# One core, Mamba block with a routed expert layer: norms applied by ScalarE, additions as identity products, a second running sum, gating on VectorE, one copy of the routed rows

## What is computed

```python
h = x + mamba(layernorm(x, g1, b1))            # expand to 512 channels, 16 states per channel
m = gelu(layernorm(h, g2, b2) @ mlp_w1.T + mlp_b1) @ mlp_w2.T + mlp_b2
x = layernorm(x + (h + m))                     # no gain, no bias
# expert layer: softmax over 8 experts, the two best of each token
routed = sum over the two: weight * down_e(silu(gate_e(x)) * up_e(x))
shared = silu(x @ sg.T) * (x @ su.T) @ sd.T
out = layernorm(x + routed + shared)

# mamba: xz = x @ in_proj.T; causal convolution of 4 taps on half of it, silu -> xc
# dt, B, C from xc; the recurrence for each channel d and state n:
#   h = exp(dt * A[d, n]) * h + dt * xc * B[n];   y += C[n] * h
# y = (y + xc * D_param) * silu(z);  y @ out_proj.T
```

## Time and profile before

| | us |
|---|---|
| median of 3 executions | 6505.38 (6500.32 to 6505.66) |
| the profiled execution | 6514.27 |
| its span, first to last instruction | 6512.5 |
| mean granted TensorE clock | 0.770 |
| VectorE busy | 4832.9 (74%) |
| GpSimd busy | 4603.2 (71%) |
| TensorE busy (matmul) | 4338.0 (67%) |
| ScalarE busy | 2740.6 (42%) |

### The profile page before, as it was taken

How to read it: one execution, slowest core, us unless ns; L and a number is a source line. 1 busy time by engine, 2 the same in 40 slices (tenths; PEclk the granted TensorE clock), 3 DMA queues, 4 the chain that set the end, 5 groups by cost and what they waited for, 6 DMA issues and landing times. The chain is left out here.

```text
span 6512.5 us, 72002 instructions
## 1 busy us (share of the span) xinstructions
PE 4338.0 (67%) x18880; PEld 3104.8 (48%) x18880; DVE 4832.9 (74%) x7430; ACT 2740.6 (42%) x4258; POOL 4603.2 (71%) x2862
## 2 busy tenths in 40 slices
PE   4566666667767766667776666777666677676653
PEld 2344444455545544445554544555445455454543
DVE  5877888888877778777777777878877778777521
ACT  3444444444444433444444444444344443444211
POOL 4577766666666677876667787766777867787644
PEclk7576777778778878778877777887878888887876
DMA  6755211122222222332222233221234322343345
GB/s 183 219 183 187 91 36 36 35 62 80 80 80 67 67 67 67 96 97 75 64 69 50 82 105 92 72 68 56 57 107 115 83 87 72 114 127 91 98 111 137
DMA packets 361969, 596.83 MB, mean 92 GB/s; under 512 B 36560, under 2 KB 184272, under 8 KB 361440
## 3 DMA queue, kind: packets, MB, share of 16 engines
q1 hardware_dynamic: 312416, 524.97, 26.4%
q0 software_dynamic: 49152, 67.27, 5.1%
HBM read 372.60 MB, written 219.50 MB: 91 GB/s over the span
## 5 line engine op out<-in xcount | busy, mean ns | idle before, releaser
L473 POOL TENSOR_TENSOR dBx<-dtx,Bbc 128x1024 f32<-128x1024 f32 x1024 | 2434.3, 2409 | 806.4 <-DVE hs L978 767.4
L978 DVE TENSOR_TENSOR_SCAN hs<-ps,dBx 128x512 f32<-128x512 f32 x2048 | 2420.0, 1208 | 255.0 <-issue 135.8
L759 PE MATMUL ps<-ident,hs 128*128 128x128 f32 x8192 | 1601.1, 346 | 874.6 <-DVE acc L992 485.2
L626 ACT ACTIVATE ps<-dt,A 128x512 f32<-128x512 f32 x2048 | 1400.3, 689 | 1323.8 <-DVE hs L978 1307.2
L759 PEld LDWEIGHTS ps<-ident,hs 128*128 128x128 f32 x8192 | 1250.3, 180 | 1282.7 <-DVE acc L992 680.9
L992 DVE SCALAR_TENSOR_TENSOR acc<-ps,C_tok,acc 128x512 f32<-128x512 f32 x1920 | 1368.4, 734 | 554.1 <-PE ps L759 530.1
L907 PE MATMUL ps<-post_tmp,wx 128*128 128x128 f32 x2560 | 453.4, 343 | 118.1 <-issue 118.0
L543 POOL DMA_INDIRECT fx<-Y_slots,slots x256 | 406.7, 1589 | 170.3 <-DMA fx<-shared 86.3
L907 PEld LDWEIGHTS ps<-post_tmp,wx 128*128 128x128 f32 x2560 | 427.0, 254 | 151.1 <-issue 145.8
L526 POOL DMA_INDIRECT X_slots<-xs,slots x256 | 255.1, 996 | 260.0 <-DVE slots L1117 178.9
L888 PE MATMUL ps<-ident,xin 128*128 128x128 f32 x640 | 152.3, 383 | 340.3 <-DMA xin<-X_slots 339.8
(11 more groups left out here) (148 smaller groups left out, 5773.0 us busy)
## 6 DMA issues: line engine op xcount, KB each, us to landing
Bbc<-B_scratch SPq DMA_DIRECT2D x512, 256.0 KB
wx<-in_experts SPq DMA_DIRECT2D x320, 384.0 KB
X_slots<-xin SPq DMA_DIRECT2D x26, 2056.0 KB, 19.7
Y_slots<-xin SPq DMA_DIRECT2D x26, 2048.0 KB
xin<-X_slots SPq DMA_DIRECT2D x320, 128.5 KB
Y_slots<-mT SPq DMA_DIRECT2D x320, 128.0 KB
xt<-in_x SPq DMA_DIRECT2D x32, 512.0 KB, 4.0
shared<-xt SPq DMA_DIRECT2D x32, 512.0 KB
```

What stands on the lines that cost most here:

```text
L473: pool.tensor_tensor(dBx[u % 3][:], dtx[b % 2][:, 2 * h:2 * h + 2, :], Bbc[g % NBB][:, n % CH:n % CH + 1, :].broadcast_to([P, 2, T]), ALU. ...
L626: act.activation(psA[s % 2][:], dt[b % 2][:, j, :], ACT.Exp, scale=A[:, j, n:n + 1]).then_inc(s_dA, 1)
L759: i = pe.transpose(psH[w % 2][:, j * P:(j + 1) * P], hs[(n * CT + j) % NHB][:, t * P:(t + 1) * P], ident[:])
L978: dve.tensor_tensor_scan(hs[s % NHB][:], psA[s % 2][:], dBx[s // 2 % 3][:, s % 2, :], 0.0, ALU.mult, ALU.add).then_inc(s_scan, 1)
```

## The change

- The norms are applied by ScalarE (`activation` Identity with scale = rs and bias = -mean*rs, four for each norm). GpSimd keeps the statistics' small steps and gets one more pair for each norm (the negated mean, its product with rs). The second norm is written once.
- Additions move to TensorE: `c*D` is a product with a diagonal matrix `D_diag` (made once) in the PSUM bank of y; `x`, `h1`, `b2` and the normed row of the shared expert come in as products with the identity or with a row of ones ahead of the accumulating products. VectorE's three residual sums go. ScalarE copies the first (`h1`) and the last (`shared`) out of PSUM; the second isn't written at all, and VectorE's statistics and ScalarE's norm read it in PSUM.
- States 0 to 7 and 8 to 15 go to two running sums, both opened by ScalarE (`OPENED = (0, 8)`), in three buffers; both are turned into the same PSUM bank and so added. VectorE weighs 14 states in place of 15.
- The gate product moves from GpSimd to VectorE and reads y in PSUM.
- There is one copy of the routed rows. The four scatters of the second choice wait until the first four have landed and until GpSimd has put the second weight into column 256.
- The clearing DMAs, the store of `shared` and the store of the output are issued by ScalarE's queue in place of SyncE's.
- All places of `AT` are new.

The diff, cut to its core (of the tables only some rows):

```diff
-    "DVE_scan": [-1.02, -0.66, 0.44, 0.54, 0.61, 0.61, 0.61, 1.13, 1.33, 1.57, 4.26, 6.08, 8.14, 8.17, 9.47, 9.55,
...
-        56.28],
-    "SP_clear": [-37.09, -36.96, -35.8, -35.8, -35.8, -15.26, -9.9, 16.04, 16.04, 28.1, 38.4, 42.27, 44.02],
+    "ACT_clear": [-149.74, -149.74, -120.5, -63.13, -61.58, -58.78, -56.39, -44.7, -42.62, -42.37, -29.56, -28.54,
+        -18.41],
+    "ACT_pre": [-43.32, -35.45, -31.95, -30.73, -26.98, -25.74, -24.71, -23.66, -22.94, -22.51, -21.59, -18.98,
+        -17.83, -15.8, -12.47, -11.93, -11.8, -6.18, -6.18, -2.27, -1.06, -1.06],
+    "DVE_scan": [-2.42, -2.42, 4.13, 4.13, 4.19, 4.35, 5.02, 5.02, 5.02, 5.22, 5.51, 8.41, 10.2, 10.2, 12.09, 12.09,
...
+        45.14, 45.7, 46.72, 47.13, 49.01, 49.01, 49.98, 50.63, 51.65, 52.14, 55.9, 58.19, 60.69, 61.76, 63.68, 63.68,
+        63.68],
+    "POOL_pre": [-57.58, -7.07, 1.08],
+    "POOL_post": [103.49, 108.76, 117.68, 125.35, 125.35, 125.45, 128.45, 129.69, 130.77, 131.01, 131.01],
...
+    OPENED, NACC = (0, NS // 2), 3
...
             def pre():
...
+                    pool.tensor_scalar(nb["pre"][:], mv["pre"][:, :, 0], -1.0, None, ALU.mult).then_inc(s_var_pre, 1)
...
+                    pool.tensor_tensor(nb["pre"][:], nb["pre"][:], rs["pre"][:], ALU.mult).then_inc(s_rstd_pre, 1)
-                    for t in range(NTB):
...
-                        pool.tensor_scalar(tok_pre[b % 2][:, t, :], xt[b % NX_IN][:, t, :], mv["pre"][:, t, 0:1],
-                                           rs["pre"][:, t:t + 1], ALU.subtract, ALU.mult).then_inc(s_norm_pre, 1)
...
                     for c in range(2):
+                        if c:
+                            yield b
+                            pool.wait_ge(s_scattered, (b * 2 + 1) * NTB * 16)
+                            pool.tensor_scalar(xs[:, :, D], top2[:], 1.0, None, ALU.mult).then_inc(s_second, 1)
...
+            def clear():
+                for i, rows in enumerate((X_slots[0], X_slots[1], Y_slots[0], Y_slots[1])):
+                    width = 2 * rows.shape[1]
+                    for k in range(CLEARS):
+                        yield i
...
+                        act.dma_start(rows.rearrange("(p n a) d -> p n (a d)", p=P, a=2)[:, k * n:(k + 1) * n, :],
...
+                        act.activation(tok_pre[b % 2][:, t, :], x[:, t, :], ACT.Identity, scale=rs["pre"][:, t:t + 1],
+                                       bias=nb["pre"][:, t:t + 1]).then_inc(s_norm_pre, 1)
...
+                        act.activation(h1[:, 2 * q:2 * q + 2, :], psG[q][:].rearrange("p (t d) -> p t d", d=D),
+                                       ACT.Copy).then_inc(s_h1, 1)
...
+                        act.activation(x[:, 2 * q:2 * q + 2, :], psY[:].rearrange("p (t d) -> p t d", d=D),
+                                       ACT.Copy).then_inc(s_sum, 1)
...
+                    act.dma_start(shared[b], x[:].rearrange("p t d -> p (t d)")).then_inc(s_kept, 16)
...
+                        pe.matmul(psY[:], D_diag[:, j, :], c[:, j, :], start=True, stop=False, skip_group_check=True)
                         for t in range(NTB):
-                            i = pe.transpose(psY[:, t * P:(t + 1) * P], acc[b % 2][:, t, j * P:(j + 1) * P], ident[:])
+                            for n in OPENED:
+                                i = pe.matmul(psY[:, t * P:(t + 1) * P], sums(b, n)[:, t, j * P:(j + 1) * P], ident[:],
+                                              is_transpose=True, start=False, stop=(t, n) == (NTB - 1, OPENED[-1]),
+                                              skip_group_check=True)
...
+                                if k == 0:
+                                    pe.matmul(psG[q][:, t * D:(t + 1) * D], ident[:], x[:, 2 * q + t, :], start=True,
+                                              stop=False)
...
+                                if k == 0:
+                                    o = psG[q][:, t * D:(t + 1) * D]
+                                    pe.matmul(o, one_row[:], b2[:], start=True, stop=False)
+                                    pe.matmul(o, ident[:], x[:, 2 * q + t, :], start=False, stop=False)
+                                    pe.matmul(o, ident[:], h1[:, 2 * q + t, :], start=False, stop=False)
...
+                            pe.matmul(psY[:, t * D:(t + 1) * D], ident[:], h1[:, 2 * q + t, :], start=True, stop=False)
...
-                        dve.scalar_tensor_tensor(out=c[:, j, :], in0=c[:, j, :], scalar=D_half[:, j:j + 1],
-                                                 in1=psY[:], op0=ALU.mult, op1=ALU.add).then_inc(s_y_plus, 1)
-                    for q in range(2):
-                        yield b
-                        dve.wait_ge(s_out_mm, per_batch(b, q, 2))
...
-                        dve.tensor_tensor(h1[:, 2 * q:2 * q + 2, :], psG[q][:].rearrange("p (t d) -> p t d", d=D),
-                                          x[:, 2 * q:2 * q + 2, :], ALU.add).then_inc(s_h1, 1)
...
+                        dve.wait_ge(s_silu_z, per_batch(b, j, CT))
+                        dve.tensor_tensor(c[:, j, :], psY[:], post_tmp[:, j, :], ALU.mult).then_inc(s_gated, 1)
```

More of the change, by code:

```diff
@@ L197, in build @@
         dbc = sb("dbc", [NX, T])[:]
-        xs = [sb(f"xs{i}", [P, NTB, ROW]) for i in range(2)]
-        h1 = xs[0][:, :, 0:D]
+        xs = sb("xs", [P, NTB, ROW])
+        h1 = xs[:, :, 0:D]
         mT = sb("mT", [P, KD, T])
@@ L646, in post @@
                         act.activation(post_tmp[:, j, :], psG[j % 2][:], ACT.Tanh, scale=0.5).then_inc(s_tanh_z, 1)
+                    for q in range(2):
+                        yield b
+                        act.wait_ge(s_out_mm, per_batch(b, q, 2))
+                        if q == 0 and b:
+                            act.wait_ge(s_scattered, b * 2 * NTB * 16)
+                            act.wait_ge(s_down_s, b * 2)
+                        act.activation(h1[:, 2 * q:2 * q + 2, :], psG[q][:].rearrange("p (t d) -> p t d", d=D),
+                                       ACT.Copy).then_inc(s_h1, 1)
+                    for t in range(NTB):
+                        yield b
+                        if t == 0:
+                            act.wait_ge(s_rstd_post, (b * 2 + 1) * 2)
+                            act.wait_ge(s_gated, (b + 1) * CT)
+                        act.activation(tok_post[:, t, :], psG[t // 2][:, t % 2 * D:(t % 2 + 1) * D], ACT.Identity,
+                                       scale=rs["post"][:, t:t + 1], bias=nb["post"][:, t:t + 1]).then_inc(s_norm_post, 1)
                     for k in range(KD):
@@ L659, in post @@
                             s_gelu, 1)
+                    for t in range(NTB):
+                        yield b
+                        if t == 0:
+                            act.wait_ge(s_rstd_post, (b + 1) * 4)
+                            act.wait_ge(s_m2_mm, (b + 1) * 2)
+                        act.activation(xs[:, t, 0:D], psG[t // 2][:, t % 2 * D:(t % 2 + 1) * D], ACT.Identity,
+                                       scale=rs["post"][:, t:t + 1], bias=nb["post"][:, t:t + 1]).then_inc(s_norm_post, 1)
                     for k in range(KD):
@@ L693, in results, with finish @@
                                            scale=xin[p % 2][:, i, D:ROW]).then_inc(s_yo, 1)
+            def finish():
+                for b in range(PERIODS):
+                    for f in fins_in[b]:
+                        for t in range(NTB):
+                            yield b
+                            if t == 0:
+                                act.wait_ge(s_rstd_fin, (f + 1) * 2)
+                            act.activation(fx[:, t, :], fx[:, t, :], ACT.Identity, scale=rs["fin"][:, t:t + 1],
+                                           bias=nb["fin"][:, t:t + 1]).then_inc(s_norm_fin, 1)
+                        act.wait_ge(s_norm_fin, (f + 1) * NTB)
+                        act.dma_start(out[f].rearrange("(t p) d -> p t d", p=P), fx[:]).then_inc(s_stored, 16)
             weave((scan(), AT["ACT_scan"]), (weigh(), AT["ACT_weigh"]), (pre(), AT["ACT_pre"]),
-                  (post(), AT["ACT_post"]), (experts(), AT["ACT_experts"]), (results(), AT["ACT_results"]))
+                  (post(), AT["ACT_post"]), (experts(), AT["ACT_experts"]), (results(), AT["ACT_results"]),
+                  (finish(), AT["ACT_finish"]), (clear(), AT["ACT_clear"]))
+            act.wait_ge(s_stored, 16 * NB)
         @block.tensor
@@ L937, in _ @@
             dve.wait_ge(s_consts, CONSTS)
+            dve.wait_ge(s_halved, 5)
+            for j in range(CT):
+                dve.tensor_scalar(D_diag[:, j, :], ident[:], D_half[:, j:j + 1], None, ALU.mult).then_inc(s_diag, 1)
             dve.wait_ge(s_A_exp, 1)
@@ L982, in weigh @@
                 for b in range(NB):
-                    for n in range(1, NS):
+                    for n in range(NS):
+                        if n in OPENED:
+                            continue
                         for t in range(NTB):
                             w = (b * NS + n) * NTB + t
```

(2 more changed lines are left out.)

340 lines of the change are left out of this document (149 added, 191 removed), and 30 rows, old and new, of the table AT.

## The result

The changed kernel takes 6632.2 us (median of 4 runs, 6627.5 to 6637.3) against 6505.1 us for the kernel before, 1.0197 times as long, 95% interval 1.0179 to 1.0215. The forecast was 6105 with a range to 6350. So the sign was wrong, and the size by 527 us.

The account below looks back on a forecast made before the run. No engine was full; VectorE's work plus the waits of its in-order stream were taken to set the time. Terms -231 - 248 - 72 + 30 + 30 + 0 + 110 - 20 = -401 gave 6105 us, range 5890 to 6350.

Parts of the forecast that it names:

- TensorE's work: Added products, 15 us a batch at most, cancel against shorter waits for GpSimd's norms: 0, bounds -200 and +300.
- The waits that the additions were set against: TensorE's idle for GpSimd's norms, 228.9 and 167.1 us in all, 12 us per batch, was to shrink.
- The relief as a whole: The terms for VectorE, gap, finishing batches, scatters, ScalarE and tail taken together: -511 us.
- scatters: On GpSimd, the second four scatters wait for the first four to land: +30 us, bounds 0 and 166.
- VectorE's work: Less weighing, no residual sums, cheaper c*D, all counted as time: -231 us, bounds 0 to -231.
- The gap between batches: The 24.6 us without a scan between two batches shrinks by the new order: -248 us, bounds 0 and -372.
- GpSimd and the finishing batches: GpSimd's lighter work saves 6 us in each of 12 finishing periods: -72 us, bounds 0 and -126.
- late exps: In ScalarE's in-order stream, norms waiting for statistics hold the scans: +30 us, bounds 0 and +96.
- The start: Clears on ScalarE's queue delay the first scan (+65) and the next three batches (+45): +110 us, bounds 0 and +364.
- The tail: After the last scan, shorter norms and a shorter post stage: -20 us, bounds 0 and -40.
- Rival (C): TensorE becomes the bound, turns of scans queueing behind post products: +399 us, 6905, chance 0.08.
- The sign that I named for being wrong: Gap still over 20 us, TensorE past 85% of a period with growing turn waits, or late ScalarE exps.

Follow-up runs that it names:

- e1: The changed kernel without all of TensorE's added products (their sums missing from the output): 6255.0 us, ratio 0.9609.
- e7: The kernel before, with twelve idle identity products a batch put ahead of its second MLP products, output unchanged: 6677.9 us, ratio 1.0268.
- e3: The changed kernel with the 52 clearing DMAs issued by SyncE again, at their old places: 6577.2 us, ratio 1.0104.
- h1: The changed kernel with clears on SyncE and the second residual sum back on VectorE and GpSimd, output complete: 6379.5 us, ratio 0.98.

## Why the prediction was wrong, step by step

**TensorE's work: the step that failed.** It read "I let the two cancel: 0", with bounds -200 and +300. The two were added products, 15 us a batch as an upper value, against waits for GpSimd's norms. Measured, the additions alone are +377 us (e1): nine tenths of the added work in the path, where the upper bound had two thirds. What the shorter waits gave back no run separates. Two errors are in it. First, I judged the cost by TensorE's share of a whole period (132.3 of 187.9) and did not cut the period at the stage that gets the products, where e1 and e7 show almost every added microsecond in the path. Second, the count: "20 products of 256 columns (0.379)" took one instruction for each, while the groups show two (x256 for four products a batch in 32 batches). Groups of the changed kernel:

```profile
L869 PE MATMUL ps<-b,one_row 1*128 1x256 f32 x256 | 88.8, 426 | 11.3 <-ACT post_tmp L658 11.3
...
L871 PE MATMUL ps<-xs,ident 128*128 128x256 f32 x256 | 76.2, 379 | 0.0
...
L820 PE MATMUL ps<-xc,D_diag 128*128 128x512 f32 x256 | 131.0, 593 | 0.7 <-ACT mT L708 0.7
```

L829 in the earlier trace rows said the same (x1024 for 16 products in 32 batches). The 15 us a batch still came out near, 418 / 32 = 13.1 in e1, because the union of overlapping records is well below the sum of their durations. That is luck: two records a product were left out, and the overlap was too. In the chain a product took 0.53 us and not 0.379.

**The waits that the additions were set against** did go: no wait of TensorE for GpSimd's norms is left, and it waits 67.2 and 34.7 us for ScalarE's, in place of 228.9 and 167.1. What that was worth is part of e1's time and not measured by itself.

**The relief as a whole: sign right, size 60%.** VectorE, gap, finishing, scatters, ScalarE and tail were to give -511 us. e1 less e3's 55 us for the clears would be 6200, so -305 was got, if the two effects add up (no run has both edits). So the miss of 527 us has two main parts, TensorE's 377 and 206 of missing relief, less 55 that the clears cost under their forecast. This sum closes by the way it is made and proves nothing further.

**VectorE's work: right in its groups, less in time.** Weighing lost 80 us of 94 and the three sums went. But the busy time, a union in which neighbours overlap, fell by only 151 us, and h1 shows that putting one sum back costs some 8 us. "I take all of it" was too much.

**The gap between batches: right as a gap, not as time.** At the boundary after the batch above, VectorE runs these scans:

```profile
3288.43 1.21 DVE L1024 TENSOR_TENSOR_SCAN hs<-ps,dBx 128x512 f32<-128x512 f32 x1
...
3302.59 1.22 DVE L1024 TENSOR_TENSOR_SCAN hs<-ps,dBx 128x512 f32<-128x512 f32 x1
...
3317.46 3.45 DVE L1024 TENSOR_TENSOR_SCAN hs<-ps,dBx 128x512 f32<-128x512 f32 x3 [1.19 <-ACT ps L609]
...
3325.59 4.54 DVE L1024 TENSOR_TENSOR_SCAN hs<-ps,dBx 128x512 f32<-128x512 f32 x4
```

The first of the three scans at 3317.46 is the last of its batch (the starts of every 64th scan show it) and the other two open the next, so nothing stands between the batches, and 4.7 us without a scan follow where there were 24.6. But the longest break now lies inside the batch: 12.9 us from the end of the 57th scan (3288.43) to the 58th (3302.59), with the routing and its wait of 5.99 us for the ranks in it. The order was also not quite what the prediction read from the table: the second of the next batch's dt steps (3316.66 on GpSimd) runs behind four scatters and not ahead of seven.

The -248 did not follow. In e1, where no addition interferes, the period of batch 8 is

```profile
1496.50:1677.60 181.10, 133.91 (x590) 96.08 (x590) 141.94 (x212) 95.55 (x153) 97.57 (x58) 0.79 0.22 72
```

so VectorE is idle 39.2 us in it, against 36.5 in batch 8 before and 187.9 - 147.9 = 40.0 in batch 9. As means by kind of period (without experts, with them, with finishing) VectorE is idle 32.3, 38.2 and 47.4 us before and 30.2, 38.6 and 38.3 in e1. The idle time of the gap did not go; it stands elsewhere in the period, and only the finishing periods lost some. This is read from the profiles; a kernel with the old gap and all else new would need a table of its own and was not tried.

**GpSimd and the finishing batches: right in size.** GpSimd is busy 3583.6 (forecast 3500 to 3600). A finishing period was 14.6 us above a plain one and is 7.7, that is 6.9 less where 6 were forecast.

**ScalarE: right in work, its wait misplaced.** It is busy 3140.8 us (near 3160). A norm took 0.56 to 0.59 us where 0.5 was taken. What the forecast feared, late exps, is 126.2 us in all (92.1 before). What it did not price are the copies that VectorE's statistics wait for, 203.8 us.

**The start: mechanism right, size half.** +55 us in time (e3), +110 forecast. The first part (+65) came as 51 (57 by e3). The +45 for the next batches did not come: a clear that stood alone held the queue 0.38 us, and only in a burst did it cost more (the four from 107.68 held it 0.38, 0.60, 3.45 and 6.34 us). The Trainium skill (DMA: Bandwidth & Descriptors, section Issuing engines are not separate DMA queues) calls the sequencer's time to initiate a DMA usually small beside the transfer. For the clears that stood alone the trace agrees; for the burst it does not, where eight issues held ScalarE 37.53 us.

**The tail: right**, -38 within its bounds, at twice the -20 taken.

**Rival (C)** had the place and the sign, and 0.08. It made TensorE the bound through turns queued behind post products, and decided at 85% of a period. Neither holds: the batch-8 period stands at 149.4 of 194.8, 77%, and the waits for turns fell. What decides is a chain, not a load. Its price (+399) missed too: it took 480 for the added work where 377 came, 110 for the start where 55 came, and nothing for the gap and the finishing periods. The sign that I named for being wrong would not have shown it.

Beside this stands a rule of the Trainium skill (Perfetto Trace Analysis, sections Identifying the Most-Contended Engine and Optimization Strategy): the engine with the highest occupancy is to be optimized first, within each regime where a kernel has several, and for TensorE the shares of its weight loads and of peak arithmetic are to be taken, not that of its matmuls. Before the change VectorE's busy share was the highest beside the weight loads', over the span (74% against 48%) and in the stretch of batch 4 (81% against 54%). Taking 151 us of work from it still came with a loss, because the share does not say who waits for the work where it goes. The waits of VectorE above say it.

## What to carry to other kernels

Before moving work to the engine with spare time, cut the period at the stage that will hold it and ask who waits for the result: twelve products cost 6.4 us a batch ahead of the MLP's and 0.5 ahead of the turns of the scans. The MLP's residual sum, made by VectorE on the way out of PSUM with GpSimd preparing the other operand, cost some 8 us in all; as identity products in front of the main product it cost 206. Where an in-order engine waits for a small result, look at what stands ahead of that result on the other engine: one reordering gave 108 us with no work removed. And a break that is closed in one place has to be looked for in the others before its time is counted as gained.

## What the runs showed of the hardware that was not expected

A VectorE subtraction of eight values took 3.04 us in a stretch where GpSimd works on 128x1024 operands. VectorE's row, then GpSimd's, of the changed kernel:

```profile
2520.90 3.04 DVE L1185 TENSOR_TENSOR m<-count,cap 1x8 f32<-1x8 f32 x1
```

```profile
2521.57 2.34 POOL L443 TENSOR_TENSOR dt<-dt,dtx 128x1024 f32<-128x1024 f32 x1
```

It ends at 2523.94, and GpSimd's at 2523.91. Eight instances of this line are in the trace. In six of them it lasts 3.04 to 3.09 us, starts while GpSimd issues a scatter, and ends 0.03 us after the GpSimd addition that follows (L443). In the other two it lasts 0.15 us, and beside it GpSimd only issues gathers. The whole line costs 18.6 us. That it waits for GpSimd is inferred from the ends; it starts 0.7 us before the addition does, and the rows do not say why it was not through by then. The Trainium skill (Trainium Architecture — The Big Picture, section What this means for kernel authors) says that within SBUF's engine side VectorE and GpSimd share ports under an exclusive lock. These rows fit that, and no run here tests it.
